# Splitting the shared experts' down product into three rounded products, and moving four experts' weight splits into the routed stage

## The reference, cut to what matters

```
h = layernorm(x) * (1 + cb) + sb
probs = softmax(h @ w_router); top 4 of 16 experts, weights made to sum to 1
g   = silu(h @ we1) * (h @ we3) * cw          # per expert, 256 -> 128
moe = sum over experts of g @ we2              # 128 -> 256
shared = (silu(h @ ws1) * (h @ ws3)) @ ws2     # 256 -> 512 -> 256
x = x + gb * (shared / 5 + moe * 4 / 5)
```

## Time and profile before

| | us |
|---|---|
| median of 3 runs (344.13 to 345.23) | 345.16 |
| the profiled execution, whole | 345.19 |
| its span (first to last instruction) | 343.5 |
| PE busy in the span | 326.6 |
| DVE busy | 257.1 |
| POOL busy | 202.2 |
| ACT busy | 196.2 |

### The profile page before, as it was taken

One profiled execution on the slowest core, in us unless ns is written; L12 is line 12 of the kernel. 1 busy time (PEld: TensorE's weight loads), 2 busy tenths in 40 slices (PEclk: granted clock), 3 DMA queues, 4 the chain that ended last, 5 costly groups with the idle time before them and its releaser, 6 DMA issues.

```text
span 343.5 us, 7753 instructions
## 1 busy us (share of the span) xinstructions
PE 326.6 (95%) x2260; PEld 299.7 (87%) x2260; DVE 257.1 (75%) x794; ACT 196.2 (57%) x440; POOL 202.2 (59%) x285
## 2 busy tenths in 40 slices
PE   8998899989999999999999998999999999999995
PEld 4787789979899898988878877999999999998884
DVE  0889999798988887465899757666566666669796
ACT  2467778665866755665444325666666666666210
POOL 2578846531688667457777500666666666667810
PEclk9999999998999999999999999999999999999999
DMA  7314830000112149873232254787766665989935
GB/s 260 109 50 171 262 121 18 15 20 13 72 77 96 73 160 349 281 222 120 105 118 98 81 145 134 234 255 228 236 211 199 198 194 164 327 314 333 360 105 172
DMA packets 42264, 57.55 MB, mean 168 GB/s; under 512 B 5128, under 2 KB 34576, under 8 KB 42224
## 3 DMA queue, kind: packets, MB, share of 16 engines
q1 hardware_dynamic: 34272, 35.42, 33.4%
q0 software_dynamic: 6864, 19.80, 15.1%
q10 hardware_dynamic: 1088, 1.84, 1.7%
HBM read 32.64 MB, written 24.40 MB: 166 GB/s over the span
## 4 chain that ended last, share of the span: by engine, by line
PE 68%; DVE 17%; issue 7%; ACT 4%; DMA 1%; POOL 1%; DVEq 0%; ACTq 0%
PE ps L1779 15%; PE ps L1780 14%; PE ps L1781 14%; PE ps L1953 7%; PE ps L2155 4%; PE ps L2181 2%; DVE negmax L1598 2%; PE ps L1967 2%; PE ps L1786 1%; PE ps L2055 1%; DMA wmod_sb<-in_L_wmod_dram 1%; DVE bn L1185 1%; PE ps L1888 1%; DVE y_in L1472 1%; DVE rpool L1591 1%
## 5 line engine op out<-in xcount | busy, mean ns | idle before, releaser
L806 POOL DMA_INDIRECT y_rows<-y_sb,aside x72 | 71.1, 987 | 52.2 <-ACT y_sb L1081 41.0
L767 POOL DMA_INDIRECT xg_rows<-hrow,slot_u x64 | 66.4, 1038 | 22.1 <-issue 18.3
L1779 PE MATMUL ps<-rpool 128*128 128x256 f32 (+3 forms) x152 | 50.5, 332 | 3.3 <-DVE rpool L1209 1.4
L1779 PE MATMUL ps<-w_hi_routed,xT_hi 128*128 x158 | 45.1, 286 | 2.2 <-DVE xT_lo L1715 2.2
L1780 PE MATMUL ps<-rpool 128*128 128x256 f32 (+3 forms) x152 | 46.5, 306 | 0.0
L1781 PE MATMUL ps<-rpool 128*128 128x256 f32 (+3 forms) x152 | 46.5, 306 | 0.0
L1780 PE MATMUL ps<-w_lo_routed,xT_hi 128*128 x158 | 44.7, 283 | 0.0
L1781 PE MATMUL ps<-w_hi_routed,xT_lo 128*128 x158 | 44.7, 283 | 0.0
L1072 ACT ACTIVATE r_silu<-ps 128x256 f32<-128x256 f32 x40 | 15.4, 385 | 37.0 <-PE ps L1781 35.2
L1779 PEld LDWEIGHTS ps<-rpool 128*128 128x128 f32 x152 | 29.5, 194 | 6.6 <-DVE rpool L1209 3.1
L1779 PEld LDWEIGHTS ps<-w_hi_routed,xT_hi 128*128 128x128 f32 x158 | 30.2, 191 | 2.9 <-issue 2.7
(11 more groups left out here) (236 smaller groups left out, 938.6 us busy)
## 6 DMA issues: line engine op xcount, KB each, us to landing
xs<-xg_rows SPq DMA_DIRECT2D x68, 144.0 KB
y_in<-y_rows SPq DMA_DIRECT2D x16, 512.0 KB, 5.4
xg_rows<-empty SPq DMA_DIRECT2D x4, 576.0 KB, 3.7
x_in<-in_L_attn_x_dram SPq DMA_DIRECT2D x16, 128.0 KB, 2.1
w_raw_routed<-in_L_ffn_we_dram SPq DMA_DIRECT2D x8, 256.0 KB, 5.1
xs_own<-xg_rows SPq DMA_DIRECT2D x11, 144.0 KB
wmod_sb<-in_L_wmod_dram ACTq DMA_DIRECT2D x3, 512.0 KB, 6.8
out_dram<-x SPq DMA_DIRECT2D x12, 128.0 KB, 1.8
```

The costliest lines, as they stand in the source:

```text
L767: nc.gpsimd.indirect_dma_start(out=xg, out_offset=bass.IndirectOffsetOnAxis(ap=slot_u[:, t, k:k + 1].bitcast(U32), axis=0), in_=hrow[:, t, ...
L806: nc.gpsimd.indirect_dma_start(out=yb, out_offset=bass.IndirectOffsetOnAxis(ap=dest[:, 2 * n + i:2 * n + i + 1].bitcast(U32), axis=0), in_ ...
L1779: nc.tensor.matmul(dst, w[0], x_[0], start=first, stop=False)
```

## The change

1. `down(n)` for units 4 to 11 is done as three rounded products, as `gate_up` is: high by high, high by low, low by high, so 12 fp32r matmuls of 256 columns in place of 4 float32 ones. Units 0 to 3 and 12 to 15 stay.
2. For it ScalarE makes `w2_hi()` once (128x1024, at n = 3) and `g_hi(n)` for each of the eight units (128x512), VectorE `w2_lo()` once (at n = 4) and `g_lo(n)` for each of the eight (128x512, at the end of what it does for the unit). `g_lo` waits for `g_hi`, `g_hi` for `g_step`, `down(n)` for `g_lo(n)`.
3. Experts 12 to 15 are split no longer between the shared units but in pieces behind the first six pairs' work: one piece of 512 elements behind pairs 0 to 3, two of 256 behind pairs 4 and 5 (`split_late`, on ScalarE and VectorE). The first pair waits for 12 experts, pair 6 for the late pieces.
4. The experts 0 to 11 stand in other places of the two `splits` tables.

```diff
+LATE_SPLITS = {0: [(12, 0, W2)], 1: [(13, 0, W2)], 2: [(14, 0, W2)], 3: [(15, 0, W2)],
+               4: [(12, W2, WX), (13, W2, WX)], 5: [(14, W2, WX), (15, W2, WX)]}
...
+            def w2_hi():
+                act.wait_ge(s_ld_s, 5 * 16)
+                act.wait_ge(s_wvo_lo, B)
+                nc.scalar.activation(w_hi_s[:, :, W2:WX], w_raw_s[:, :, W2:WX], ACT.Copy).then_inc(s_w2_hi, 1)
+            def g_hi(n):
+                act.wait_ge(s_g, n + 1)
+                nc.scalar.activation(g_hi_s[:, n % 2, :], act_g[:, n % 2, :], ACT.Copy).then_inc(s_ghi, 1)
...
+            def split_late(n):
+                for e, first, end in LATE_SPLITS.get(n, []):
+                    act.wait_ge(s_ld_w[LOAD_OF[e]], 5 * 16)
+                    nc.scalar.activation(w_hi_r[:, e, first:end], w_raw_r[:, e, first:end], ACT.Copy
+                                         ).then_inc(s_whi_late, 1)
...
-            splits = {3: [0, 1], 4: [2, 3], 5: [4, 5], 6: [6, 7], 7: [8, 9], 8: [10, 11], 9: [12], 10: [13, 14], 11: [15]}
+            splits = {3: [0, 1], 4: [2], 5: [3], 6: [4, 5], 7: [6], 8: [7, 8], 9: [9], 10: [10], 11: [11]}
...
                 for e in splits.get(n, []):
                     split_routed(e)
+                if n >= SH:
+                    g_hi(n)
...
+            def g_lo(n):
+                dve.wait_ge(s_ghi, n - SH + 1)
+                nc.vector.tensor_tensor(g_lo_s[:, n % 2, :], act_g[:, n % 2, :], g_hi_s[:, n % 2, :].bitcast(F32),
+                                        ALU.subtract).then_inc(s_glo, 1)
...
-            splits = {4: [0, 1, 2], 5: [3, 4], 6: [5, 6], 7: [7, 8, 9], 8: [10, 11], 9: [12], 10: [13, 14], 11: [15]}
+            splits = {4: [0, 1], 5: [2], 6: [3, 4], 7: [5, 6], 8: [7, 8], 9: [9], 10: [10], 11: [11]}
...
+                if n == SH:
+                    w2_lo()
                 for e in splits.get(n, []):
                     split_routed(e)
+                g_lo(n)
...
+                if SH <= n < UNITS_FIRST:
+                    pe.wait_ge(s_w2_lo, 1)
+                    pe.wait_ge(s_glo, n - SH + 1)
...
+                    nc.tensor.matmul(to, hi, w2_hi, start=begun, stop=False, skip_group_check=True)
+                    nc.tensor.matmul(to, hi, w2_lo_s[:, e, :], start=False, stop=False, skip_group_check=True)
+                    last = nc.tensor.matmul(to, lo, w2_hi, start=False, stop=(e == SH - 1), skip_group_check=True)
...
-                    pe.wait_ge(s_whi_r, E)
-                    pe.wait_ge(s_wlo_r, E)
+                    pe.wait_ge(s_whi_r, FIRST_LATE)
+                    pe.wait_ge(s_wlo_r, FIRST_LATE)
+                if n == FIRST_LATE // 2:
+                    pe.wait_ge(s_whi_late, 2 * (E - FIRST_LATE))
+                    pe.wait_ge(s_wlo_late, 2 * (E - FIRST_LATE))
```

More of the change, by code:

```diff
@@ L503, in adaln_block @@
             "gate_up_mm", "down_mm", "silu", "g", "shared_gated", "shared_added"))
+        s_w2_hi, s_w2_lo, s_ghi, s_glo = (sem(n) for n in ("w2_hi_shared", "w2_lo_shared", "g_hi", "g_lo"))
+        s_whi_late, s_wlo_late = sem("w_hi_late"), sem("w_lo_late")
         s_xs = [sem(f"xs_loaded{n}") for n in range(RING)]
@@ L1050, in _ @@
                     norm2_rows(TILES - 1)
+                    w2_hi()
                 if n == 2:
@@ L1096, in _ @@
                     y_rows(n - 2)
+                split_late(n)
             for n in range(UNITS_FIRST + 1, UNITS_SH):
@@ L1423, in split_shared, with w2_lo @@
                                         ALU.subtract).then_inc(s_wlo_s, 1)
+            def w2_lo():
+                dve.wait_ge(s_w2_hi, 1)
+                nc.vector.tensor_tensor(w2_lo_s[:], w_raw_s[:, :, W2:WX], w_hi_s[:, :, W2:WX].bitcast(F32),
+                                        ALU.subtract).then_inc(s_w2_lo, 1)
+            def g_lo(n):
+                dve.wait_ge(s_ghi, n - SH + 1)
+                nc.vector.tensor_tensor(g_lo_s[:, n % 2, :], act_g[:, n % 2, :], g_hi_s[:, n % 2, :].bitcast(F32),
+                                        ALU.subtract).then_inc(s_glo, 1)
             def split_routed(e):
@@ L1429, in split_routed, with split_late @@
                                         ALU.subtract).then_inc(s_wlo_r, 1)
+            def split_late(n):
+                for m, (e, first, end) in enumerate(LATE_SPLITS.get(n, [])):
+                    dve.wait_ge(s_whi_late, sum(len(LATE_SPLITS[i]) for i in range(n)) + m + 1)
+                    nc.vector.tensor_tensor(w_lo_r[:, e, first:end], w_raw_r[:, e, first:end],
+                                            w_hi_r[:, e, first:end].bitcast(F32), ALU.subtract
+                                            ).then_inc(s_wlo_late, 1)
             def g_step(n):
@@ L1951, in down @@
                     tok = slice(j * P, (j + 1) * P)
-                    last = nc.tensor.matmul(to, unit(n)[1][:, tok], w_raw_s[:, e, W2:WX],
-                                            start=(e == 0 and b < NB - 1 and j % 2 == 0), stop=(e == SH - 1),
-                                            skip_group_check=True)
+                    begun = e == 0 and b < NB - 1 and j % 2 == 0
+                    if not SH <= n < UNITS_FIRST:
+                        last = nc.tensor.matmul(to, unit(n)[1][:, tok], w_raw_s[:, e, W2:WX],
+                                                start=begun, stop=(e == SH - 1), skip_group_check=True)
+                        continue
+                    hi, lo = g_hi_s[:, n % 2, tok], g_lo_s[:, n % 2, tok]
+                    w2_hi = w_hi_s[:, e, W2:WX]
+                    nc.tensor.matmul(to, hi, w2_hi, start=begun, stop=False, skip_group_check=True)
+                    nc.tensor.matmul(to, hi, w2_lo_s[:, e, :], start=False, stop=False, skip_group_check=True)
+                    last = nc.tensor.matmul(to, lo, w2_hi, start=False, stop=(e == SH - 1), skip_group_check=True)
                 if BT - 1 in tiles or n == UNITS_SH - 1:
```

4 lines of the change are left out of this document (added).

## The result

The changed kernel takes 347.19 us, the median of 7 runs (346.02 to 347.77), against 344.38 for the kernel before (7 runs, 342.84 to 345.23). The ratio is 1.0078, 95% interval 1.0057 to 1.0099. So it is slower by some 0.8%, or 2.7 us. The forecast was 345.25, no change, and its range ended at 346.5: it was wrong. (Its base, 345.19, was the profiled execution of the kernel before, 0.8 above the median of the seven, so the miss in the difference, 2.8 in place of 0.06, is larger than the 1.9 between the two totals.) Two of the executions further down, 362.96 us of b1_places_first and 358.98 us of b4_all_orders, ran at a mean granted clock of 0.85 and are left out of the ratios.

What follows compares the result with a forecast made beforehand. It took VectorE, full and level with TensorE, to bound the shared stage: 0.68 us later less 0.62 won back gives +0.06, late pieces nothing, so 345.19 + 0.06 = 345.25 us; range 344.3 to 346.0, with tails 344.0 to 346.5.

Steps and rivals of the forecast that it cites:

- VectorE's cost: Shared stage, units 5 to 9: four g_lo more and two routed splits fewer lengthen VectorE's list by 0.68 us.
- TensorE's waits: Shared stage: tile_values at 175.71 waiting about 1.0 us, about 0.3 ahead of down(6), about 1 us ahead of down(8).
- What reaches the end of the shared stage: At gate_up(12): down(8) starts 0.68 later, TensorE wins back 0.62, so everything behind comes 0.06 us later.
- TensorE's gain of eight downs: Units 4 to 11: each down takes 1.44 instead of 1.73 us, 2.3 in all, lost to waits for VectorE.
- ScalarE: Shared stage: w2_hi and eight g_hi of about 0.6 us each stay hidden, by 0.2 us at the least.
- The late pieces: First six routed pairs: pieces fit VectorE's and ScalarE's idle time, delay nothing over 0.1 us, and are taken at nothing.
- Rival 2: First six pairs: late pieces not hidden because they overrun idle time or engines wait for each other; 347.3 us, chance 0.08.
- Rival 1: Shared stage: VectorE isn't the bound, so downs 5 to 9 gain 1.45 us, giving 343.7; chance 0.12.
- rival 3: Shared stage: g_lo held by GpSimd's sends through the shared SBUF port, or sends late; 347.2 us, chance 0.06.
- Rival 4: TensorE's downs: the three products don't get cheaper because 12 weight loads don't overlap; given no chance of its own.
- VectorE's shift: Shared stage: how much later VectorE's list runs by unit 9, 0.68 us, with ends 0.60 and 1.00.

Runs made afterwards that it cites:

- b1_places_first: Changed kernel with per-pair late-piece waits and two expert splits moved earlier, plus tile places computed before the first shared addition into x; ratio 0.9979 to the kernel before.
- b4_all_orders: b1_places_first and b2_handover together, first shared addition one unit later, late pieces reordered over pairs 1 to 6 with matching waits; 341.72 us, ratio 0.9897 to before.
- a3_down_alone: Only the rounded downs added to the kernel before; all 16 experts still split in the shared stage, first pair waits for 16; ratio 1.0085 to before.
- a5_late_by_pair: a2_late_alone, but pair 6 waits for six of the eight late pieces and pair 7 for all eight; ratio 0.9992 to the kernel before.
- a1_wait_by_pair: The changed kernel, but pair 6 waits for six late pieces and pair 7 for all eight; 345.68 us, ratio 1.0015 to the kernel before.
- a6_after_again: The changed kernel itself, unaltered, profiled once more; one execution of 349.34 us.
- b5_full_precision: b4_all_orders with the eight shared downs in full float32 and without their roundings and remainders on ScalarE and VectorE; 341.16 us, ratio 0.9891 to before.
- a2_late_alone: Only the late pieces, their split tables and the single wait at pair 6 added to the kernel before; downs in full float32; ratio 1.0092 to before.
- b2_handover: Changed kernel with per-pair late-piece waits and two expert splits moved earlier, plus first pairs' rows and register load moved up on VectorE and ScalarE; ratio 0.9941 to before.

## Why the prediction was wrong, point by point

- **VectorE's cost: right.** `g_step(5)` to `g_step(9)` took 21.07 us, before 20.40: 0.67 more, where 4 x 0.61 less 2 x 0.88 gave 0.68. Rows of VectorE's timeline, `g_step(5)`, a `g_lo` and `g_step(9)`:

```profile
167.74 0.69 DVE L1490 SCALAR_TENSOR_TENSOR act_g<-act_g,ps 128x512 f32<-128x512 f32 x1 [0.32 <-ACT act_g L930]
...
188.21 0.68 DVE L1468 TENSOR_TENSOR g_lo_shared<-act_g,g_hi_shared 128x512 fp32r<-128x512 f32 x1
188.81 0.67 DVE L1490 SCALAR_TENSOR_TENSOR act_g<-act_g,ps 128x512 f32<-128x512 f32 x1
```

- **TensorE's waits: right.** `tile_values` at 174.89 + 0.81 = 175.70 (forecast 175.71) with a wait of 0.96 (about 1.0); `down(8)` behind 0.81 (about 1). The waits of 0.3 ahead of `down(5)` and `down(6)` were over-counted: 0.16 and none.
- **What reaches the end of the shared stage: right.** `gate_up(12)` 36.86 us from the mark, before 36.79, so +0.07 against +0.06, behind an idle of 0.28 (197.24 + 0.12 to 197.64) against 0.3. TensorE's gain of eight downs is lost as reckoned; a3_down_alone shows how it would be with all the splits left in.
- **ScalarE: right.** No wait of TensorE or VectorE for a `g_hi` in after's shared stage (units 4 to 12).
- **The late pieces: this step failed.** "So nothing is delayed by more than 0.1 ... Taken at nothing" held for the first five of the six pairs (silu periods of 2.81 up to pair 5) and not for the sixth (5.03), which is also the sign of being wrong that the prediction named, a pair of over 2.9 between 210 and 225. The step compared the pieces with idle time on VectorE and ScalarE, 1.05 and 0.84 us, and that was right: a5_late_by_pair shows that they fit. It didn't ask who waits for the last of them, and from when. "TensorE reads a pair's products only behind the next pair's gate and up" is true of `gT_lo`, but the wait for the pieces stands ahead of the gate and up of pair 6, right behind the work of pair 5 on TensorE. The sum could have been made from the earlier trace rows and the order of the calls: VectorE starts a pair's products 0.42 us behind the start of the silu (217.81 to 218.23), works 2.81 - 1.05 = 1.76, and then up to 0.8 for two pieces, so it is done 2.98 behind the silu. TensorE starts the next gate and up one period of 2.81 behind the start of the last one, and the silu begins when gate and up, 1.44 us, is over: TensorE is ready 1.2 to 1.4 us behind the silu's start. That is a wait of some 1.7 us; measured 1.98, so the term put at nothing was 2.2 us in the period, and more where the clock fell behind it. It was also not asked whether the pieces are of use to pair 6: the last two of the eight are the down parts of experts 14 and 15, and a1_wait_by_pair shows that pair 6 can do without them.
- **Rival 2** had the sign, its chance was 0.08, and its price (2 to 4 us) covered what came. But its mechanism was another, a piece that doesn't fit between the pairs; the wait by count was in the diff, and it named nothing from it. That its price fits is luck.
- **Rival 1** fell with the shared stage, **rival 3** with `g_lo` at 0.68 beside GpSimd's sends. **Rival 4**: the three products come 0.12 apart.
- **The range** (344.0 to 346.5) was made from VectorE's shift and the spread of the runs; the failed step had no term in it. The first trace has 2.4 to 2.5 us of loss at full clock in this stretch, and the medians 2.8; the mean granted clock of the seven runs was 1.00 once (346.02 us), 0.995 four times, and 0.99 twice (347.45 and 347.77), as in a6_after_again (0.99, 349.34). The last section shows that 0.995 is one fall of the clock, which the kernel before has as well at 77 us, and 0.99 two; so these two probably had the one behind the stop too. How much of the median it makes can't be read without the traces of the timed runs.

## What to carry to other kernels

When work is moved into the gaps of another engine, reckon two things: whether it fits the gap, and when the *last* piece is done against the first instruction that waits for it; a semaphore that counts pieces makes the consumer wait for all ahead of it in the list, used or not. Let each consumer wait for its own pieces, in the order of their use: here this one wait is 0.6% (1.0078 to 1.0015). And where one engine's list is full, first look at its order (what stands ahead of that for which another engine waits); here this gave 1.0% (0.9992 of a5_late_by_pair to 0.9891 of b5_full_precision, both with full-precision downs), while the operation that the change made cheaper gave about 1 us in the traces and nothing that the runs can tell.

## What the runs showed of the hardware

A stop of TensorE can cost more than its length. Behind a wait of 1.98 us the granted clock fell to the 1.2 GHz level in two of three profiles (0.53 in a2_late_alone at once, 0.50 in a6_after_again after nine matmuls, not at all in the first profile of after), with matmuls 0.21 us apart in place of 0.12 for about 3 us, and 1.6 us lost on top of 2.2 (3.8 in all over two periods, in both). Behind the waits of 1.59 to 1.66 us at pair 1 no run showed it, and no run without the wait ahead of pair 6 showed it there. TensorE had been busy all through the stretch ahead of that wait in all three (3.00 of 3.00 us from 217 to 220). What decides between the executions stays open: the same kernel showed both.

A fall of the same kind stands in the part of the kernel that nothing here changes. Part 2 of the pages (the granted clock in 40 slices of the span, in tenths, 9 being 90% or more) shows it in the tenth slice of before, not in a3_down_alone, and in a2_late_alone only the one behind the wait:

```profile
PEclk9999999998999999999999999999999999999999
PEclk9999999999999999999999999999999999999999
PEclk9999999999999999999999999899999999999999
```

In the kernel before the granted clock is 0.57 from 77 to 81 us, with matmuls of 256 columns 0.21 apart; in a3_down_alone it is 1.00 in the same stretch. Eight of the twelve profiles have this fall, and a2_late_alone, a3_down_alone, a5_late_by_pair and b2_handover don't. TensorE's longest stop in the 5 us ahead of it is 0.87 us in the kernel before and 0.71 in the first profile of after, and in a3_down_alone, where the clock stays full, 0.72. So a stop of 2 us is not needed for a fall, and here too it isn't shown what decides. The falls can be counted from the mean of an execution, by these profiles: none leaves 0.997 to 1.00, one 0.993 to 0.995, wherever it lies (77 us in the kernel before, 222 in a2_late_alone), two leave 0.99 (a6_after_again); no profile has 0.992, which a few runs show. None of the 64 timed runs of the kernel before in the experiments is under 0.992. Of the 28 that a1_wait_by_pair was compared with, the seven at 0.997 or more have a median of 343.24 us and the other 21 one of 345.07, so 1.8 us of the spread of this kernel's times go with it. The mark stands at 161.2 us in the mean of the eight profiles with it and at 160.1 in the four without.
